# Convolution and whitening on one core: the DRAM scratch laid out by unit, the output stored as whole tiles

## The chip, the cores and the metric

The kernel runs on one core of a Trainium2 chip. The metric is device time in microseconds, from the start of the program to its end.

## The reference, cut to what matters

The input `x` is float32 of shape (4, 64, 256, 256): four images of 64 channels. Layer 0 is a long convolution: for each channel, a separable filter `hx * hy` (made by a small network of sines) is convolved with the 256 x 256 image by FFT with zero padding, and `x * bias` is added. Layer 1 whitens the 64 channels against each other:

```python
x1 = jnp.transpose(x, (1, 0, 2, 3)).reshape(64, -1)
x1_s = x1[:, ::9]                      # every ninth pixel
mean1 = jnp.mean(x1_s, axis=-1, keepdims=True)
cov = x1_s @ x1_s.T / x1_s.shape[1] + 0.01 * eye
deconv = isqrt_newton_schulz(cov, 5)
out = deconv @ (x1 - mean1)            # back to (4, 64, 256, 256)
```

Whitening needs the covariance of the whole result of layer 0 before its first output can be made, and that result (67 MB) doesn't fit on the core. So it goes to DRAM and comes back.

## The kernel before, in words

**Units.** The convolution is done in 128 units (`UNITS`), one for a channel `c` of one sweep; a sweep is two of the four images. A unit's input is a tile of 128 partitions x 1024 floats: partition `p` holds row `p` and row `128 + p` of both images (two images x two halves x 256 columns), which the host has put together, so `x[q]` is one contiguous 512 KB. On the partitions, the Toeplitz matrices of the filters are made from a Hankel load of 256 KB (L206 to L214). TensorE multiplies by the row filter (`make_v`) and then by the column filter (`make_y`), eight groups of matmuls for a unit in all (L593 to L603). VectorE adds `x * bias` and writes `y_sb[q % 2]`, one of only two buffers (L477, `finish_y`). From there, GpSimd masks every ninth pixel (L337), VectorE sums the groups (L485), and SyncE stores the tile to the scratch `convolved` (`y_dram`, L216 to L223).

**The waits on `y_sb`.** `finish_y(q)` waits until the store of unit `q - 2` has landed (`y_stored[k]`). SyncE's `load_x(q + 4)` waits until unit `q - 1` is done (L203); behind it on the same queue stand `store_y(q - 1)`, `load_hankel(q + 5)` and, from unit 68 on, `load_kept(q)`. All DMAs are issued by SyncE, so all stand in one hardware queue.

**Between.** After the last unit come the second half of the covariance on TensorE (L630), five Newton-Schulz steps (L552 to L671) and the whitening matrix `dmat`. DVE's last unit (L508 to L521) waits for the store of unit 125 (L516) and then works in two halves.

**Tiles.** The whitening runs over 64 tiles of 128 partitions x 2048 floats (1 MB). A partition is one channel of one half of an image, so `dmat` is block-diagonal with `deconv` twice. A tile is multiplied by `dmat` (L687), ScalarE and VectorE add the mean term from PSUM (L409, L578), and SyncE stores it. Fourteen tiles (`KEPT`) are loaded in the second sweep in four pieces each (L230 to L239), six more just after the last unit (L268 to L279), and the other 44 one by one as a slot comes free (L281 to L284). There are four output buffers.

**The scratch before.** `y_dram` has a row for each (image, half, channel), 128 x 256 floats, the rows of that half in order. A unit's store takes, from each partition, four runs of 1 KB (one for each image and half), and a tile's load takes 8 KB from each row. A tile's output is stored by two DMAs of 64 partitions (one for each half, L260 to L265), each partition to its place in the final array, 8 KB at a time.

The lines that the prediction's steps touch: L204 (x load), L214 (Hankel load), L223 (store of a unit), L239 (kept pieces), L258 (tile loads), L265 (output stores), L477 and L509 (VectorE's result of a unit), L516 (the wait for the store of unit 125), L598 to L601 (a group of matmuls), L630 (covariance), L687 (matmuls of a tile).

Of the kernel before, what the change touches and what calls it, by code (L numbers as in the profile page):

```python
# [6 lines left out]
F32 = mybir.dt.float32  # L7
# [36 lines left out]
ZW = 2 * C + 1  # L44
X_SLOTS, T_SLOTS, H_SLOTS = 5, 3, 3

TROWS = 8
TW = TROWS * S
TILES = B * (P // TROWS)
KEPT = 14  # L50
PIECES = 4
O_SLOTS = 4
MASK_COLS = 288


def conv_whiten(nc, x, first, hidden, columns, bias, out):
    g_dram = nc.dram_tensor("filters", [2 * C, GLEN], F32, kind="Internal").ap()
    y_dram = nc.dram_tensor("convolved", [B * HB * C, P * S], F32, kind="Internal").ap()

    with ExitStack() as ctx:  # L60
        def sb(name, shape, dt=F32):
# [96 lines left out]
        def wait(eng, s, value):  # L158
            if value > 0:
                eng.wait_ge(s, value)  # L160
# [27 lines left out]
        @block.sync  # L188
        def _(sp):
            sp.dma_start(first_sb, first).then_inc(params_loaded, 16)  # L190
            sp.dma_start(col[:], columns).then_inc(params_loaded, 16)

            sp.wait_ge(w_zeroed, 1)
            for k in range(2):
                h = slice(k * ORDER, (k + 1) * ORDER)
                sp.dma_start(w_sb[h, :, h], hidden[h, :].rearrange("p (l n) -> p l n", l=3)
                             ).then_inc(params_loaded, 16)

            def load_x(q):
                if q >= UNITS:  # L200
                    return

                wait(sp, y_done, q - X_SLOTS + 1)  # L203
                sp.dma_start(x_sb[q % X_SLOTS], x[q]).then_inc(x_loaded[q % X_SLOTS], 16)  # L204

            def load_hankel(q):  # L206
                if q >= UNITS:
                    return
                k = q % H_SLOTS

                wait(sp, flipped, q - H_SLOTS + 1)
                wait(sp, t_lo_done, q - H_SLOTS + 1)
                src = bass.AP(tensor=g_dram.tensor, offset=(q % C) * GLEN, ap=[[1, P], [C * GLEN, 2], [1, S]])
                sp.dma_start(hankel[k], src).then_inc(hankel_loaded[k], 16)  # L214

            def store_y(q):  # L216
                if q < 0:
                    return
                k = q % 2
                wait(sp, y_done, q + 1)  # L220
                dst = bass.AP(tensor=y_dram.tensor, offset=(q // C) * BLOCKS * C * P * S + (q % C) * P * S,
                              ap=[[S, P], [C * P * S, BLOCKS], [1, S]])
                sp.dma_start(dst, y_sb[k].rearrange("p (i w) -> p i w", w=S)).then_inc(y_stored[k], 16)  # L223

            def tile_in(t, lo, hi):
                image, rows = t // (P // TROWS), t % (P // TROWS)
                return bass.AP(tensor=y_dram.tensor, offset=image * HB * C * P * S + rows * TW + lo,
                               ap=[[P * S, HB * C], [1, hi - lo]])

            def load_kept(q):  # L230
                n = q - (C + 4)
                if not 0 <= n < KEPT * PIECES:
                    return
                w = TW // PIECES
                lo = n % PIECES * w

                for k in range(2):
                    sp.wait_ge(y_stored[k], 16 * (C // 2))
                sp.dma_start(kept[:, n * w:(n + 1) * w], tile_in(n // PIECES, lo, lo + w)).then_inc(kept_loaded, 16)  # L239

            for q in range(4):
                load_x(q)
            sp.dma_start(bias_sb[:], bias.to_broadcast([P, C])).then_inc(bias_loaded, 16)

            sp.wait_ge(filt_ready, 1)
            sp.dma_start(g_dram, filt).then_inc(filt_stored, 16)
            sp.wait_ge(filt_stored, 16)
            for q in range(5):
                load_hankel(q)

            for q in range(UNITS):
                load_x(q + 4)
                store_y(q - 1)
                load_hankel(q + 5)
                load_kept(q)

            def load_tile(t):
                sp.dma_start(t_in[t % slots], tile_in(t, 0, TW)).then_inc(t_loaded[t % slots], 16)  # L258

            def store_tile(t):  # L260
                image, rows, k = t // (P // TROWS), t % (P // TROWS), t % O_SLOTS
                for h in range(HB):
                    dst = bass.AP(tensor=out.tensor, offset=image * C * S * S + h * P * S + rows * TW,
                                  ap=[[S * S, C], [1, TW]])
                    sp.dma_start(dst, t_out[k][h * C:(h + 1) * C, :]).then_inc(t_stored[k], 16)  # L265


            sp.wait_ge(y_mm, UNITS)  # L268
            for t in range(KEPT, after_v):
                load_tile(t)  # L270
            store_y(LAST)
            for t in range(after_v, after_y):
                load_tile(t)
            for k in range(2):
                sp.wait_ge(y_stored[k], 16 * (UNITS // 2))
            sp.wait_ge(masked_done, LAST)
            sp.wait_ge(z_last_done, PER)
            for t in range(after_y, slots):
                load_tile(t)  # L279

            for t in range(TILES):  # L281
                if t + slots < TILES:
                    sp.wait_ge(t_mm[1], t + 1)
                    load_tile(t + slots)  # L284

                sp.wait_ge(t_act, t + 1)
                sp.wait_ge(t_dve, t + 1)
                store_tile(t)
            for k in range(O_SLOTS):
                sp.wait_ge(t_stored[k], 16 * HB * (TILES // O_SLOTS))  # L290

        @block.gpsimd
        def _(pool):
# [57 lines left out]
        @block.scalar  # L351
        def _(act):
            def flip(q):
                if q >= UNITS:
                    return
                k, h = q % T_SLOTS, q % H_SLOTS
                act.wait_ge(hankel_loaded[h], 16 * (q // H_SLOTS + 1))

                wait(act, y_mm, q - T_SLOTS + 1)
                nc.scalar.copy(t_f32[k], hankel[h][:, :, :P - 1:-1])  # L360
                nc.scalar.copy(t_hi[k], hankel[h][:, :, ::-1]).then_inc(flipped, 1)  # L361

            def round_x(q):
                if q >= UNITS:
                    return
                k = q % X_SLOTS
                act.wait_ge(x_loaded[k], 16 * (q // X_SLOTS + 1))

                wait(act, v_mm, q - 1)
                nc.scalar.copy(x_hi[q % 2], row_block(k, 0)).then_inc(x_hi_done, 1)  # L370

            def round_v(q):
                k = q % 2
                wait(act, v_mm, q + 1)

                wait(act, y_mm, q - 1)
                nc.scalar.copy(v_f32[k], ps_v[k][:, :, S:2 * S])  # L377

                nc.scalar.copy(v_hi[k], ps_v[k][:, :, 0:S]).then_inc(v_hi_done, 1)  # L379

            act.wait_ge(rate_ready, 1)
            nc.scalar.activation(decay, pos, ACT.Exp, scale=rate[:]).then_inc(decay_ready, 1)
            round_x(0)
            for layer in range(3):
                act.wait_ge(f_dve, layer + 1)
                nc.scalar.activation(hid, arg, ACT.Sin).then_inc(f_sin, 1)
            round_x(1)
            flip(0)
            flip(1)

            for q in range(UNITS):
                round_v(q)
                round_x(q + 2)
                flip(q + 2)

            act.wait_ge(filt_zeroed, 2)
            nc.scalar.activation(small[:, 7:8], small[:, 7:8], ACT.Sqrt)
            act.wait_ge(n_mm, 1)
            nc.scalar.activation(small[:, 1:2], ps[:, 0, 0:1], ACT.Sqrt).then_inc(n_act, 1)
            act.wait_ge(n_act, 1)  # L400
            nc.scalar.activation(small[:, 3:4], small[:, 1:2], ACT.Sqrt).then_inc(n_act, 1)
            act.wait_ge(d_ready, 1)

            for t in range(TILES):
                act.wait_ge(t_mm[0], t + 1)

                wait(act, t_stored[t % O_SLOTS], 16 * HB * (t // O_SLOTS))
                src = ps[:, bank(t, 0):bank(t, 0) + 2, :].rearrange("p r n -> p (r n)")
                nc.scalar.activation(t_out[t % O_SLOTS][:, 0:TW // 2], src, ACT.Identity,  # L409
                                     bias=small[:, 6:7]).then_inc(t_act, 1)  # L410

        @block.vector
        def _(dve):
# [159 lines left out]
            for t in range(TILES):  # L573
                dve.wait_ge(t_mm[1], t + 1)

                wait(dve, t_stored[t % O_SLOTS], 16 * HB * (t // O_SLOTS))
                src = ps[:, bank(t, 1):bank(t, 1) + 2, :].rearrange("p r n -> p (r n)")
                nc.vector.tensor_scalar(t_out[t % O_SLOTS][:, TW // 2:TW], src, small[:, 6:7], None, ALU.add  # L578
                                        ).then_inc(t_dve, 1)
# [139 lines left out]
```

## Time and profile before

| | us |
|---|---|
| median of 3 runs | 998.5 |
| lowest and highest | 994.86 and 1002.09 |
| the profiled execution | 994.94 |
| its span, first to last instruction | 993.1 |
| mean granted TensorE clock in it | 0.981 |

The rows below are in us of one profiled execution, counted from its first instruction. The span holds three stages: filters and ramp (0 to 41), the units (41 to 662), and from the last unit to the end (662 to 993). Of these the last holds the covariance and Newton-Schulz steps up to about 702, then the tiles. The chain of waits is one path only: what ended last, followed back.

### The profile page before, as it was taken

Reading aid. Unit: us, or ns where it says so; the run is one execution under the profiler, and the core shown is the slowest. Engines: PE = TensorE matmul, PEld = TensorE weight load, DVE = VectorE, ACT = ScalarE, POOL = GpSimd, SP = SyncE. Lnnn points to the kernel's source line nnn. Section 1 sums busy time; section 2 is a strip of 40 time slices with the busy share of each in tenths; the row PEclk is TensorE's granted clock in tenths of the full one; section 3 lists DMA queues with packets and bytes.
Section 4 is the critical chain, followed back from the end, with each engine's and each line's share of the span. In section 5 each row is a group of like instructions: output and inputs, shape, how many; then the busy total and the mean of one; then the engine's idle time right before and its main releaser. Section 6 shows DMA issues by size and latency. Waiting matters only on the chain.

```text
span 993.1 us, 15420 instructions
## 1 busy us (share of the span) xinstructions
PE 881.0 (89%) x5904; PEld 731.0 (74%) x5904; DVE 574.7 (58%) x642; ACT 397.8 (40%) x714; POOL 496.4 (50%) x277
## 2 busy tenths in 40 slices
PE   1799999999999999999999999977997777777896
PEld 0799999999999999999989899976432222222342
DVE  4487788778787657677767676771222222222332
ACT  2455555555555435454444444420121222222332
POOL 2488888889898747777767677760000000000000
PEclk9999999999999999999999999997799999999999
DMA  3799999999999959999999999975499999999999
GB/s 100 161 286 272 275 309 270 268 296 287 282 292 272 298 154 312 320 304 315 309 312 300 296 298 317 312 264 214 142 425 425 427 426 425 426 427 426 362 326 287
DMA packets 147301, 303.39 MB, mean 306 GB/s; under 512 B 10619, under 2 KB 109084, under 8 KB 132636
## 3 DMA queue, kind: packets, MB, share of 16 engines
q1 hardware_dynamic: 147228, 302.41, 92.1%
q8 instruction: 47, 0.77, 0.3%
q14 instruction: 26, 0.21, 0.1%
HBM read 167.96 MB, written 134.41 MB: 304 GB/s over the span
## 4 chain that ended last, share of the span: by engine, by line
PE 47%; DMA 41%; DVE 8%; SPq 2%; issue 1%; ACT 1%; POOL 0%; DVEq 0%; ACTq 0%
DMA convolved<-y_all 24%; DMA out<-z_all 14%; PE ps L601 12%; PE ps L687 10%; PE ps L598 7%; PE ps L599 7%; PE ps L600 7%; DVE y_all L477 4%; PE ps L630 3%; DMA out<-masked_all 2%; DVE z_all L578 1%; SPq L204 1%; ACT z_all L409 1%; DMA plain<-filters 0%; SPq L265 0%
## 5 line engine op out<-in xcount | busy, mean ns | idle before, releaser
L598 PE MATMUL ps<-rounded 128*128 128x256 f32 x1024 | 373.9, 365 | 24.6 <-issue 15.3
L337 POOL TENSOR_TENSOR masked_all<-y_all,mask 128x1024 f32<-128x1024 f32 x127 | 328.8, 2589 | 80.0 <-DVE y_all L477 79.7
L599 PE MATMUL ps<-rounded 128*128 128x256 f32 x1024 | 288.3, 282 | 0.0
L600 PE MATMUL ps<-rounded 128*128 128x256 f32 x1024 | 288.3, 282 | 0.0
L477 DVE SCALAR_TENSOR_TENSOR y_all<-x_all,bias_sb,ps 128x1024 f32<-128x1024 f32 x127 | 162.5, 1280 | 139.9 <-DMA convolved<-y_all 131.7
L598 PEld LDWEIGHTS ps<-rounded 128*128 128x128 f32 x1024 | 197.3, 193 | 30.7 <-issue 30.1
L308 POOL TENSOR_TENSOR rounded<-x_all,rounded 128x512 fp32r<-128x512 f32 x128 | 165.2, 1290 | 88.6 <-ACT rounded L370 87.4
L601 PE MATMUL ps<-plain,x_all 128*128 128x128 f32 x1024 | 197.9, 275 | 0.0
L599 PEld LDWEIGHTS ps<-rounded 128*128 128x128 f32 x1024 | 197.5, 193 | 0.0
L601 PE MATMUL ps<-plain 128*128 128x128 f32 x1024 | 196.7, 274 | 0.0
L600 PEld LDWEIGHTS ps<-rounded 128*128 128x128 f32 x1024 | 193.3, 189 | 0.0
L687 PE MATMUL ps<-kept,z_all 128*128 128x512 f32 x344 | 158.6, 612 | 33.3 <-ACT z_all L409 23.8
L601 PEld LDWEIGHTS ps<-plain,x_all 128*128 128x128 f32 x1024 | 158.2, 191 | 0.0
L687 PEld LDWEIGHTS ps<-kept,z_all 128*128 128x128 f32 x344 | 64.7, 194 | 126.3 <-issue 126.0
L601 PEld LDWEIGHTS ps<-plain 128*128 128x128 f32 x1024 | 157.3, 190 | 0.0
L370 ACT CAST rounded<-x_all 128x512 fp32r<-128x512 f32 x128 | 79.7, 622 | 193.0 <-DMA x_all<-x 193.0
L485 DVE TENSOR_REDUCE z_all<-masked_all 128x116 f32<-128x1044 f32 x127 | 156.7, 1234 | 0.0
L578 DVE TENSOR_SCALAR z_all<-ps,small 128x1024 f32<-128x1024 f32 x48 | 61.6, 1284 | 152.4 <-PE ps L687 94.5
L409 ACT ACTIVATE z_all<-ps,small 128x1024 f32<-128x1024 f32 x48 | 53.5, 1115 | 173.6 <-DMA out<-z_all 124.8
L377 ACT COPY plain<-ps 128x512 f32<-128x512 f32 x128 | 74.8, 584 | 105.5 <-PE ps L601 105.1
L466 DVE TENSOR_TENSOR rounded<-plain,rounded 128x512 fp32r<-128x512 f32 x128 | 93.2, 728 | 8.1 <-ACT rounded L361 8.1
L457 DVE TENSOR_TENSOR rounded<-ps,rounded 128x512 fp32r<-128x512 f32 x128 | 87.2, 681 | 14.0 <-ACT rounded L379 13.9
(98 smaller groups left out, 471.4 us busy)
## 6 DMA issues: line engine op xcount, KB each, us to landing
x_all<-x SPq DMA_DIRECT2D x128, 512.0 KB, 6.9
convolved<-y_all SPq DMA_DIRECT2D x128, 512.0 KB, 8.0
out<-z_all SPq DMA_DIRECT2D x96, 512.0 KB, 12.7
plain<-filters SPq DMA_DIRECT2D x128, 256.0 KB, 9.1
kept<-convolved SPq DMA_DIRECT2D x29, 1024.0 KB, 18.9
out<-masked_all SPq DMA_DIRECT2D x32, 512.0 KB, 12.8
kept<-convolved SPq DMA_DIRECT2D x56, 256.0 KB, 9.5
rounded<-convolved SPq DMA_DIRECT2D x9, 1024.0 KB, 18.8
```

The lines of the kernel that those rows point to most:

```text
L308: nc.gpsimd.tensor_tensor(x_lo[k], row_block(q % X_SLOTS, 0), x_hi[k].bitcast(F32), ALU.subtract).then_inc(x_lo_done, 1)
L337: nc.gpsimd.tensor_tensor(masked_of(k, 0, PER), by_image(y_sb[k]), mask_of(q // C, 0, PER), ALU.mult).then_inc(masked_done, 1)
L370: nc.scalar.copy(x_hi[q % 2], row_block(k, 0)).then_inc(x_hi_done, 1)
L457: nc.vector.tensor_tensor(v_lo[k], ps_v[k][:, :, 0:S], v_hi[k].bitcast(F32), ALU.subtract).then_inc(v_lo_done, 1)
L466: nc.vector.tensor_tensor(t_lo[k], hankel[h][:, :, ::-1], t_hi[k].bitcast(F32), ALU.subtract).then_inc(t_lo_done, 1)
L477: nc.vector.scalar_tensor_tensor(y_sb[k], x_sb[q % X_SLOTS], bias_sb[:, q % C:q % C + 1], ps_y[k].rearrange("p a n -> p (a n)"), ALU.mult, ...
L485: nc.vector.tensor_reduce(z_of(q % C), grouped(q % 2, 0, BLOCKS), AX_X, ALU.add).then_inc(z_done, 1)
L598: mm(wide, hi[:, b, cols], t_hi[k][:, f, :], start=True, stop=False)
L599: mm(wide, hi[:, b, cols], t_lo[k][:, f, :], start=False, stop=False)
L600: mm(wide, lo[:, b, cols], t_hi[k][:, f, :], start=False, stop=False)
L601: last = mm(o[:, b, m * S + P:(m + 1) * S], block1[:, b, cols], t_f32[k][:, f, :], start=False, stop=True)
L687: last = mm(ps[:, bank(t, u) + r, :], dmat, t_in[k][:, w:w + IMG], start=True, stop=True)
```

## The change

Three things change, all of them layouts in DRAM. The scratch now has 256 rows of 64 x 1024 floats (256 KB): a row stands for 64 consecutive partitions of one unit, and within it each partition's 1024 floats stand together. A unit's store is one DMA, whose DRAM side has the pattern of counts 2, 64, 1024 in place of 128, 4, 256. A tile is now two partitions' share of all units of a sweep: partition `(h, c)` of the tile holds channel `c` and two neighbouring rows of the partition half `h`. It is loaded from 128 rows at 8 KB each, as before in size. The output array of the kernel is `[64, 128, 2048]`, each tile stored by one DMA as one contiguous megabyte, and the host puts it in order at the end. The kept tiles come in 28 pieces of 512 KB (4 KB for a partition) in every second unit, in place of 56 pieces of 256 KB in every unit. The number of tiles, their size and all arithmetic are the same; the sum over channels still runs over the partitions of a half.

```diff
-TROWS = 8
-TW = TROWS * S
-TILES = B * (P // TROWS)
+ROWS = P // 2
+TROWS = 2
+TW = TROWS * XW
+SWEEP_TILES = ROWS // TROWS
+TILES = SWEEPS * SWEEP_TILES
 KEPT = 14
-PIECES = 4
+PIECES = 2
...
-    y_dram = nc.dram_tensor("convolved", [B * HB * C, P * S], F32, kind="Internal").ap()
+    y_dram = nc.dram_tensor("convolved", [SWEEPS * P, ROWS * XW], F32, kind="Internal").ap()
...
-                dst = bass.AP(tensor=y_dram.tensor, offset=(q // C) * BLOCKS * C * P * S + (q % C) * P * S,
-                              ap=[[S, P], [C * P * S, BLOCKS], [1, S]])
-                sp.dma_start(dst, y_sb[k].rearrange("p (i w) -> p i w", w=S)).then_inc(y_stored[k], 16)
+                dst = bass.AP(tensor=y_dram.tensor, offset=((q // C) * P + q % C) * ROWS * XW,
+                              ap=[[C * ROWS * XW, 2], [XW, ROWS], [1, XW]])
+                sp.dma_start(dst, y_sb[k]).then_inc(y_stored[k], 16)
 
             def tile_in(t, lo, hi):
-                image, rows = t // (P // TROWS), t % (P // TROWS)
-                return bass.AP(tensor=y_dram.tensor, offset=image * HB * C * P * S + rows * TW + lo,
-                               ap=[[P * S, HB * C], [1, hi - lo]])
+                sweep, rows = t // SWEEP_TILES, t % SWEEP_TILES
+                return bass.AP(tensor=y_dram.tensor, offset=sweep * P * ROWS * XW + rows * TW + lo,
+                               ap=[[ROWS * XW, P], [1, hi - lo]])
 
             def load_kept(q):
-                n = q - (C + 4)
-                if not 0 <= n < KEPT * PIECES:
+                n = (q - (C + 4)) // 2
+                if q % 2 or not 0 <= n < KEPT * PIECES:
                     return
...
             def store_tile(t):
-                image, rows, k = t // (P // TROWS), t % (P // TROWS), t % O_SLOTS
-                for h in range(HB):
-                    dst = bass.AP(tensor=out.tensor, offset=image * C * S * S + h * P * S + rows * TW,
-                                  ap=[[S * S, C], [1, TW]])
-                    sp.dma_start(dst, t_out[k][h * C:(h + 1) * C, :]).then_inc(t_stored[k], 16)
+                sp.dma_start(out[t], t_out[t % O_SLOTS]).then_inc(t_stored[t % O_SLOTS], 16)
...
-    out = nc.dram_tensor("out", [B, C, S, S], F32, kind="ExternalOutput").ap()
+    out = nc.dram_tensor("out", [TILES, P, TW], F32, kind="ExternalOutput").ap()
...
-    return r.results[0]["out"]
+    tiles = r.results[0]["out"].reshape(SWEEPS, SWEEP_TILES, 2, C, TROWS, PER, HB, S)
+
+    return np.ascontiguousarray(tiles.transpose(0, 5, 3, 6, 2, 1, 4, 7)).reshape(B, C, S, S)
```

The waits on `t_stored` (L290, L407, L576) count one store for each tile in place of two.

## Rows read from the trace of the kernel before

**Rows 1.** Windows: us, busy time and count of each engine, granted clock, DMA share, GB/s

```profile
41.00:341.00 300.00, 300.00 (x2601) 299.91 (x2600) 239.26 (x259) 165.33 (x325) 261.98 (x130) 1.00 0.98 282
365.00:645.00 280.00, 264.36 (x2212) 259.29 (x2210) 199.26 (x221) 135.41 (x276) 201.36 (x111) 0.99 1.00 309
684.00:702.00 18.00, 10.61 (x33) 7.68 (x34) 5.79 (x25) 0.37 (x2) 0.00 (x0) 0.57 0.01 2
730.00:920.00 190.00, 142.95 (x309) 55.87 (x307) 49.39 (x39) 42.88 (x39) 0.00 (x0) 0.99 1.01 426
930.00:985.00 55.00, 55.00 (x128) 24.09 (x128) 20.52 (x16) 18.95 (x17) 0.00 (x0) 1.00 0.98 320
```

**Rows 2.** Windows of line L477 alone: us, DVE busy (count), clock, DMA share, GB/s

```profile
41.00:141.00 100.00, 26.99 (x22) 1.00 0.99 280
...
365.00:465.00 100.00, 25.62 (x20) 1.00 1.01 314
465.00:565.00 100.00, 24.33 (x19) 0.98 1.00 303
565.00:645.00 80.00, 20.49 (x16) 1.00 0.99 309
```

**Rows 3.** The chain of waits, 592 to 668 us: start, length, what

```profile
594.03 8.76 DMA convolved<-y_all
602.80 0.02 issue
602.82 1.29 DVE y_all L477
604.13 0.35 SPq L204
604.48 0.05 issue
604.53 8.62 DMA convolved<-y_all
...
662.35 0.66 DVE y_all L509
...
667.23 15.88 PE ps L630 x116
```

**Rows 4.** The page's DMA queue: packets, MB, share of 16 engines

```profile
q1 hardware_dynamic: 147228, 302.41, 92.1%
```

**Rows 5.** The page's DMA issues: count, KB each, median us to landing

```profile
x_all<-x SPq DMA_DIRECT2D x128, 512.0 KB, 6.9
convolved<-y_all SPq DMA_DIRECT2D x128, 512.0 KB, 8.0
plain<-filters SPq DMA_DIRECT2D x128, 256.0 KB, 9.1
```

**Rows 6.** DMA in the window 5 to 12 us, in 40 slices (x loads, 4 KB runs)

```profile
GB/s 47 187 281 374 281 328 351 304 304 374 421 421 445 421 468 398 398 398 421 374 468 421 468 398 398 421 421 374 343 170 143 94 117 117 117 94 45 37 12 0
```

**Rows 7.** The store of a unit: issues and time to landing

```profile
L223 SPq DMA_DIRECT2D convolved<-y_all x128: 360/434/1462, 41.0 to 665.4; - x128
DMA to landing us min/median/max: 2.9/8.0/12.1
```

**Rows 8.** The chain of waits at the ramp, 30 to 60 us: two groups of matmuls apart, early and late

```profile
31.05 0.43 PE ps L601 x2
32.11 0.43 PE ps L601 x2
...
45.40 0.22 PE ps L601 x2
45.98 0.22 PE ps L601 x2
```

More of the change, by code:

```diff
@@ L289, in _ @@
             for k in range(O_SLOTS):
-                sp.wait_ge(t_stored[k], 16 * HB * (TILES // O_SLOTS))
+                sp.wait_ge(t_stored[k], 16 * (TILES // O_SLOTS))
         @block.gpsimd
@@ L405, in _ @@
                 act.wait_ge(t_mm[0], t + 1)
-                wait(act, t_stored[t % O_SLOTS], 16 * HB * (t // O_SLOTS))
+                wait(act, t_stored[t % O_SLOTS], 16 * (t // O_SLOTS))
                 src = ps[:, bank(t, 0):bank(t, 0) + 2, :].rearrange("p r n -> p (r n)")
@@ L574, in _ @@
                 dve.wait_ge(t_mm[1], t + 1)
-                wait(dve, t_stored[t % O_SLOTS], 16 * HB * (t // O_SLOTS))
+                wait(dve, t_stored[t % O_SLOTS], 16 * (t // O_SLOTS))
                 src = ps[:, bank(t, 1):bank(t, 1) + 2, :].rearrange("p r n -> p (r n)")
```

## The prediction

> **What bounds the kernel now.** I read the windows by stage first, then the counts of L477 (one for each unit) in the same stages, then the chain of waits, and last the DMA page.
>
> In the first sweep TensorE never stops: 300.00 us busy of 300, and the DMA share is 0.98 at 282 GB/s [rows 1]. A unit takes 4.6 us: a group of matmuls starts every 0.58 us, eight times over is 4.6 [rows 8], and 22 units in 100 us agree [rows 2]. In the second sweep the kept tiles are loaded beside the units, and TensorE is busy 264.36 of 280 us [rows 1]. Between 365 and 645 us there are 20 + 19 + 16 = 55 units, 5.09 us each [rows 2]. The chain says what holds them: the landing of a store, VectorE's 1.29 us that waited for its buffer, SyncE's 0.35 us, and again a store of 8.6 to 8.8 us [rows 3]. Two such buffers alternate, so a unit costs half of that ring. The engines of the DMA are full (share 1.00 at 309 GB/s [rows 1]), where 426 GB/s went through with 8 KB runs [rows 1]: 1 KB runs are the reason.
>
> From the last unit's first half (662.35) to the end is 331 us [rows 3]. Of these the tiles take nearly 290: DMA-bound at 426 GB/s until near 930, then TensorE-bound, 16 tiles of eight matmuls in 55 us [rows 1].
>
> **The change part by part.**
>
> *Runs of the unit's store, 1 KB to 4 KB.* By bytes alone this frees the DMA. 128 descriptors replace 512. A unit moves 1.31 MB (512 + 512 + 256 KB [rows 5]), at 282 GB/s 4.65 us; if the two big transfers went at the 421 GB/s of the x loads [rows 6] and only the 256 KB at 282, it would be 2.49 + 0.93 = 3.4 us, under TensorE's 4.6. That is the gain the edit offers if all else is equal, and it could be had only in the second sweep: 55 x (5.09 - 4.61) = 26 us.
>
> *The shape of the store.* All else isn't equal. The DRAM side's outermost count goes from 128 to 2, while the SBUF side stays 128 partitions. The question is over how many of the 16 DMA engines such a transfer is spread. The trace has no store like it, but it has one count that shows that the number can be below 16. Queue 1 moved 147228 packets [rows 4]. Data packets, one for each contiguous run, are 16384 (x) + 65536 (unit stores) + 32768 (Hankel) + 7168 (kept pieces) + 6400 (50 tiles) + 8192 (outputs) + 128 (filters out) + 33 (network input, 33 rows) + 128 + 384 + 128 (columns, hidden weights, bias) = 137249. That leaves 9979 for completions. The 624 DMAs at 16 each would make 9984. Five are missing, which is what the one DMA with 33 rows would leave if it ran on 11 engines, the largest divisor of 33 up to 16. So I read: the engines take equal shares of the outermost count, and a count that 16 doesn't divide gets fewer of them. Each side must be cut so, and 2 can be cut in two only. The two shares are 64 partitions each, 256 KB.
>
> The Trainium skill says this outright (DMA: Bandwidth & Descriptors, "Why a DMA increments its semaphore by 16 and not by 1"): the number of engines is the largest one up to 16 that divides the slowest non-1 count of both patterns. By that rule the store runs on 2; by the rule of thumb that long runs are better it would be a gain. The completion count agrees with the former for the 33 rows, but no run here yet shows it for two sides with different outer counts.
>
> *Cost on two engines.* The 16 engines pass 426 GB/s with 8 KB runs [rows 1], 26.6 each; in the window of 4 KB loads the full slices are near 421 [rows 6], 26.3 each. So the store of a unit takes 262144 B / 26.3 GB/s = 10.0 us on each of its two. The same two also carry their sixteenth of everything else: x 32768 B, 1.25 us; Hankel 16384 B in 1 KB runs, at something between 17.6 (282/16) and 26.3 GB/s, I take 22, 0.75 us. Sum 12.0 us for a unit against 4.6. The other fourteen engines are idle most of this time. Kept pieces add 32768 B, 1.25 us, 28 times: 35 us (the 56 smaller pieces before were the same bytes).
>
> Does anything hide it? TensorE's 4.6 us (8.5 at the ramp's slow pitch, 8 x 1.06 [rows 8]) and VectorE, ScalarE and GpSimd fit in 12. Nothing but the two buffers stands between the store and the chain: `finish_y(q)` waits for store q - 2, while store q - 1 is in the queue, so the two engines never run dry (the answer to a landing, 1.29 + 0.35 us plus the issue, is far shorter than a store). The new bound is those engines' throughput, not a latency. x and Hankel loads stand in the same queue behind the store and come late too, but five x slots and three Hankel slots cover one store.
>
> *Sum.* The first store is issued at 41.0 [rows 7]. The last wait on a store in this stage is L516, for the store of unit 125, the 126th. Up to its landing: 126 x 10.0 = 1260, 124 x loads x 1.25 = 155, 123 Hankel loads x 0.75 = 92, kept 35. 41 + 1542 = 1583. Then the rest as before, 331: 1914 (the 2 stores still in the queue then, 20 us on two engines, delay tiles 14 to 20, for which nobody asks before 14 kept tiles are used up). TensorE is busy a third of the time now, and its clock may stand lower: in the 18 us of small steps at 684 us it was 0.57 [rows 1]. The covariance of 15.88 us [rows 3] may take up to twice that; I take half of it, 8. With 1.9 us outside the span, and a few us for the two engines' gaps, 1930. The bounds: 26.6 GB/s for everything gives 11.7 us for a unit, about 1890, and engines somewhat quicker when fourteen are idle are not excluded; the 17.6 GB/s of the mixed first sweep for all bytes would give 17.5 us a unit (the last rival), but there most runs were 1 KB, so I go a third of the way, to 2150. 994.94 was 3.6 under the median; that is nothing here.
>
> *Kept pieces* every second unit, 4 KB runs in place of 2 KB: same bytes, half the issues, 0 to -5 us under the old bound, nothing under the new one.
>
> *Tile loads*: 8 KB runs as before, 256 KB apart in place of 128. The output stores before had just that pitch and ran within the 426 GB/s mix [rows 1]. Zero; at worst, the 44 loads' 46 MB at the second sweep's 309 GB/s in place of 426, 149 - 108 = 41 us. I take the end to which the row of the pitch belongs, 0.
>
> *Output stores*: one DMA for a tile in place of two, contiguous, 128 partitions outermost on both sides, so all 16 engines. SyncE issues 64 fewer. The stage is bound by bytes at 426 and then by TensorE, so 0; the store that ends the kernel is 1 MB either way. -2 to +2.
>
> **The rivals.**
>
> *Fast: the store is spread over 16 engines all the same* (patterns split again before they reach the chip, or the cut taken from the SBUF side alone). For it: the pattern says the same thing to a program that would split 64 again. Against it: the missing five completions. Then DMA demand is 3.4 us a unit plus 0.6 for kept pieces, TensorE sets the pace in both sweeps, and the time is 995 - 26 = 969, perhaps 973 with landing waits left over. It decides as soon as the busiest engine needs less than TensorE's 4.6 us for a unit; on four engines that would still be 5.0 + 2.0. 13%.
>
> *No change: 16 engines, but the rate of the units is set by reading and writing DRAM at once*, not by the runs. For it: the share is full at 309 GB/s beside TensorE, VectorE and all [rows 1]. Against it: loads and stores in the tile stage mix too, and pass 426 [rows 1]. The ring of two buffers then keeps its 8.6 to 8.8 us [rows 3], the unit its 5.09, and the time is 995. 6%, half of it a gain of some us over 1%.
>
> *Slower still*: two engines, and each passes only the 17.6 GB/s of the mixed first sweep. 17.5 us for a unit, 126 x 5.5 = 690 more, 2620. It is the far end of the forecast's own case, with little weight since its runs are long.
>
> **How the numbers follow.** Slow case 81%, fast 13%, little change 6%. The predicted time is 1930, and 1800 to 2150 takes in the bounds of the engines' rate and the clock; the 19% of the other cases are left out. This kernel's measurement tells about 1% from no change. Faster by over 1%: 0.15; within 1%: 0.04; slower: 0.81.
>
> **What would show it.** The median of `convolved<-y_all` to landing goes from 8.0 to over 20 us (two stores in the queue). L477 starts every 12 us, its idle time released by that DMA on nearly all of 127. The DMA share in the unit stages falls to about (2 x 12 + 14 x 2) / (16 x 12) = 0.27, GB/s to 110; queue 1's completions fall by 128 x 14 = 1792 packets, and by 1024 more for the 64 output DMAs and 448 for the 28 kept ones that go. The tiles still run at 426. The chain is nearly all `DMA convolved<-y_all` up to 1580. I'm wrong if the share in the units stays near 0.8 with landings under 8 us.

## The result, and the profile after

The changed kernel takes 1897.66 us (median of 4 runs, 1896.63 to 1898.15) against 997.81: ratio 1.901, 95% interval 1.894 to 1.908. Predicted were 1930, and 1800 to 2150.

The windows of the kernel after, with the columns of [rows 1]; the first three are of the units, then the small steps before the tiles, then the tiles:

```profile
41.00:341.00 300.00, 177.95 (x1065) 173.88 (x1063) 92.39 (x103) 66.62 (x132) 103.56 (x52) 0.80 0.41 112
365.00:645.00 280.00, 163.08 (x946) 159.39 (x946) 86.10 (x96) 60.27 (x120) 95.91 (x48) 0.78 0.37 111
700.00:1500.00 800.00, 450.24 (x2707) 440.19 (x2706) 233.91 (x261) 162.90 (x324) 238.33 (x130) 0.78 0.43 124
...
1592.00:1610.00 18.00, 10.26 (x32) 7.41 (x32) 6.18 (x26) 0.37 (x2) 0.00 (x0) 0.57 0.40 147
1640.00:1840.00 200.00, 151.86 (x335) 60.04 (x334) 53.94 (x42) 46.71 (x42) 0.00 (x0) 1.00 1.01 427
```

The DMA passes 112 GB/s where it passed 282, and TensorE's clock stands near 0.8. The tiles run at 427 GB/s as before. The whole loss is in the units. How often VectorE finishes one, in the window 60 to 335 us, and what it waited for over the whole run (us of idle time, number of times):

```profile
L476 DVE SCALAR_TENSOR_TENSOR y_all<-x_all,bias_sb,ps x23: 1279/1281/1283, 66.3 to 328.4; 128x1024 f32<-128x1024 f32 x23
```

```profile
  DMA convolved<-y_all: 1055.0, 124
```

22 intervals in 262.1 us: 11.91 us a unit, where the kernel before had 4.64 in the same window. The chain of waits, which answers to [rows 3]:

```profile
520.49 22.02 DMA convolved<-y_all
542.51 0.03 issue
542.54 1.29 DVE y_all L476
543.83 0.02 issue
543.85 0.34 SPq L207
544.19 0.04 issue
544.24 22.04 DMA convolved<-y_all
...
1571.41 0.76 DVE y_all L508
...
1576.29 15.42 PE ps L629 x116
```

A store takes 22 us to land and not 8.6, and two buffers share it: (22.02 + 1.29 + 0.34 + 0.09) / 2 = 11.9. From the last unit's first half (1571.41) to the end of the span (1895.6) it is 324 us, 7 fewer than before. The page's queue, which answers to [rows 4], and its issues:

```profile
q1 hardware_dynamic: 91228, 302.40, 48.7%
...
convolved<-y_all SPq DMA_DIRECT2D x128, 512.0 KB
...
plain<-filters SPq DMA_DIRECT2D x128, 256.0 KB, 21.9
```

The same bytes in 56000 fewer packets. Data packets are now 137249 - 49152 (unit stores) - 3584 (kept pieces) = 84513, so 6715 are completions, as the prediction calls the packets that carry no data. 532 DMAs at 16 would make 8512; the 33-row load leaves out its 5 again, and 1792 more are missing: exactly 14 for each of the 128 stores.

### The profile page after: what moved, and what is told of

Read it like the earlier page. It is cut to its first block, busy times and chain, and to the rows that moved or that the text cites. A ratio compares the mean times of both kernels' runs of the same rounds, so it can differ in the third digit from the quotient of the medians.

```text
span 1895.6 us, 15300 instructions
## 1 busy us (share of the span) xinstructions
PE 1141.6 (60%) x5904; PEld 979.2 (52%) x5904; DVE 568.6 (30%) x642; ACT 399.9 (21%) x714; POOL 491.0 (26%) x277
## 3 DMA queue, kind: packets, MB, share of 16 engines
q1 hardware_dynamic: 91228, 302.40, 48.7%
## 4 chain that ended last, share of the span: by engine, by line
DMA 84%; PE 7%; DVE 6%; SPq 2%; issue 1%; ACT 0%; DVEq 0%; ACTq 0%
DMA convolved<-y_all 74%; DMA out<-z_all 9%; PE ps L686 4%; DVE y_all L476 4%; SPq L207 2%; PE ps L629 1%; DVE z_all L577 1%; PE ps L600 0%; DVE kept L436 0%; DMA plain<-filters 0%; ACT z_all L408 0%; PE ps L665 0%; PE ps L597 0%; PE ps L669 0%; PE ps L598 0%
## 5 line engine op out<-in xcount | busy, mean ns | idle before, releaser
L597 PE MATMUL ps<-rounded 128*128 128x256 f32 x1024 | 475.1, 464 | 652.0 <-issue 638.6
L597 PEld LDWEIGHTS ps<-rounded 128*128 128x128 f32 x1024 | 267.7, 261 | 672.3 <-issue 667.4
L476 DVE SCALAR_TENSOR_TENSOR y_all<-x_all,bias_sb,ps 128x1024 f32<-128x1024 f32 x127 | 162.6, 1280 | 1056.1 <-DMA convolved<-y_all 1055.0
L598 PE MATMUL ps<-rounded 128*128 128x256 f32 x1024 | 355.1, 347 | 0.0
L599 PE MATMUL ps<-rounded 128*128 128x256 f32 x1024 | 353.1, 345 | 0.0
L600 PE MATMUL ps<-plain,x_all 128*128 128x128 f32 x1024 | 297.4, 390 | 0.0
L598 PEld LDWEIGHTS ps<-rounded 128*128 128x128 f32 x1024 | 269.9, 264 | 0.0
L599 PEld LDWEIGHTS ps<-rounded 128*128 128x128 f32 x1024 | 263.8, 258 | 0.0
L600 PEld LDWEIGHTS ps<-plain,x_all 128*128 128x128 f32 x1024 | 256.0, 305 | 0.0
L600 PE MATMUL ps<-plain 128*128 128x128 f32 x1024 | 207.1, 285 | 0.0
L600 PEld LDWEIGHTS ps<-plain 128*128 128x128 f32 x1024 | 171.2, 205 | 0.0
L465 DVE TENSOR_TENSOR rounded<-plain,rounded 128x512 fp32r<-128x512 f32 x128 | 87.9, 687 | 8.1 <-ACT rounded L360 8.1
```

The lines of the kernel that those rows point to most:

```text
L465: nc.vector.tensor_tensor(t_lo[k], hankel[h][:, :, ::-1], t_hi[k].bitcast(F32), ALU.subtract).then_inc(t_lo_done, 1)
L476: nc.vector.scalar_tensor_tensor(y_sb[k], x_sb[q % X_SLOTS], bias_sb[:, q % C:q % C + 1], ps_y[k].rearrange("p a n -> p (a n)"), ALU.mult, ...
L597: mm(wide, hi[:, b, cols], t_hi[k][:, f, :], start=True, stop=False)
L598: mm(wide, hi[:, b, cols], t_lo[k][:, f, :], start=False, stop=False)
L599: mm(wide, lo[:, b, cols], t_hi[k][:, f, :], start=False, stop=False)
L600: last = mm(o[:, b, m * S + P:(m + 1) * S], block1[:, b, cols], t_f32[k][:, f, :], start=False, stop=True)
```

## The experiments

The kernel before ran beside each group; its median was 991.45, 995.24 and 992.96 us in the three. Ratios are against it, with a 95% interval. Times of a unit are worked out as above, from the first and last start of VectorE's result of a unit (L477, or L476 to L479 by the kernel) in the windows 60 to 335 us (first sweep) and 370 to 640 us (second). With 2 and 4 parts the second sweep starts later than that, so only the first window is given for them. The code cuts leave out the waits, whose counts follow the number of stores and buffers. Where one time is given alone, the kernel ran once.

**Two DMAs of 64 partitions.** The changed kernel, scratch and runs as they are.

```diff
-                dst = bass.AP(tensor=y_dram.tensor, offset=((q // C) * P + q % C) * ROWS * XW,
-                              ap=[[C * ROWS * XW, 2], [XW, ROWS], [1, XW]])
-                sp.dma_start(dst, y_sb[k]).then_inc(y_stored[k], 16)
+                for h in range(2):
+                    dst = bass.AP(tensor=y_dram.tensor, offset=((q // C) * P + h * C + q % C) * ROWS * XW,
+                                  ap=[[XW, ROWS], [1, XW]])
+                    sp.dma_start(dst, y_sb[k][h * ROWS:(h + 1) * ROWS, :]).then_inc(y_stored[k], 16)
...
```

> The changed kernel with one edit: a unit's store is two DMAs, one for each half of 64 partitions, so that the outermost count is 64 on both sides. Scratch layout, run length (4 KB), bytes and tiles are the same. Theory A (the time is lost to the number of engines that the outermost count allows): all 16 engines take part, TensorE sets the pace of the units, L477's counterpart starts every 4.6 to 4.7 us, and the time is 960 to 980 us. Theory B (the new scratch layout is slow to write, a 256 KB stretch for each half in one place): the time stays within 5% of 1898 us, landings near 20 us.

991.61 us, ratio 0.9999 (0.9973 to 1.0025). The loss is gone with this one edit, so neither the layout nor the run length was to blame. Queue 1's 95068 packets hold 10555 completions, all that 660 DMAs make but the 5 of the 33-row load: all 16 engines took part in each half. But the gain that I expected (960 to 980) isn't there: 4.76 us a unit in the first sweep and 5.08 in the second.

**The scratch in 4, 8 and 16 parts.** The store is one DMA again; only the outermost count of its DRAM side differs (its offset, the tile loads and the host's order follow).

```diff
-ROWS = P // 2
+PARTS = 4
+ROWS = P // PARTS
...
-                              ap=[[C * ROWS * XW, 2], [XW, ROWS], [1, XW]])
+                              ap=[[C * ROWS * XW, PARTS], [XW, ROWS], [1, XW]])
...
```

> The changed kernel with the scratch cut into 4 parts of 32 partitions in place of 2 of 64: the store is still one DMA of 4 KB runs, its DRAM pattern has the counts 4, 32, 1024. Theory A: four engines carry 128 KB each, 5.0 us for the store by the 12.08 - 2.0 us that two engines took for twice as much, 7.0 us a unit with their share of the x and Hankel loads (7.3 with kept pieces), so 41 + 127 x 7.1 + 331 = 1270 to 1300 us. 12 completion packets are missing for each store, 1536 in all. Theory B (layout, or something that goes by the run length or the number of descriptors): within 5% of 1898. A third, that any outermost count under 128 is handled by 2 engines: 1898.

> The changed kernel with 8 parts of 16 partitions, pattern 8, 16, 1024: eight engines carry 64 KB each. Theory A (busiest engine's throughput): 4.83 us was the difference between 2 and 4 engines, 128 KB a unit; so 64 KB fewer gives 6.94 - 2.4 = 4.5 us in the first sweep, where TensorE's 4.61 takes over, and 7.57 - 2.4 = 5.2 in the second. Total 995 to 1015 us, with 8 completions missing for each store. Rival (the landing latency of a store on two buffers is what binds, and it doesn't fall with bytes): over 1100.

> The changed kernel with the scratch in 16 parts of 8 partitions: one DMA, counts 16, 8, 1024. Theory A: 16 engines, no completions missing, DMA demand 3.3 to 3.9 us for a unit, TensorE-bound at 4.6: 960 to 980 us, the same as with two DMAs of 64 within 3 us. Theory B: near 1898, or if the stretch of 256 KB mattered, something between.

| outermost count | total, us | a unit, first sweep | queue 1's packets | completions missing for a store |
|---|---|---|---|---|
| 2 (the change) | 1897.66 | 11.91 | 91228 | 14 |
| 4 | 1283.17 | 6.92 | 91484 | 12 |
| 8 | 1040.09 | 5.09 | 91996 | 8 |
| 16 | 976.35 | 4.62 | 93020 | 0 |

16 parts: ratio 0.9852 (0.9811 to 0.9893). The row of L477 with 4 parts, and with 16:

```profile
L477 DVE SCALAR_TENSOR_TENSOR y_all<-x_all,bias_sb,ps x39: 1279/1280/1282, 66.1 to 329.1; 128x1024 f32<-128x1024 f32 x39
```

```profile
L477 DVE SCALAR_TENSOR_TENSOR y_all<-x_all,bias_sb,ps x60: 1269/1281/1283, 62.4 to 334.8; 128x1024 f32<-128x1024 f32 x60
```

For 2, 4, 8 and 16 the number of engines is the outermost count, and the missing completions count the idle ones; the pace of the units follows it. The times with 4 and with 8 parts are of one run each. Four parts came out as expected. Eight did not: 1040 where I had 995 to 1015, 5.09 us where the busiest engine's sum gave 4.5. Its chain in the first sweep:

```profile
203.49 8.51 DMA convolved<-y_all
212.03 1.29 DVE y_all L477
213.72 8.16 DMA convolved<-y_all
```

(8.51 + 1.29 + 0.4) / 2 = 5.1: the chain goes around the ring of two buffers, and its landings of 8.2 to 8.5 us are longer than the near 7.3 (2 x 4.5 less 1.7) that the busiest engine's sum would make them. The last experiment comes back to that.

**The output alone.** The kernel before with the tiles stored whole.

```diff
...
-                for h in range(HB):
-                    dst = bass.AP(tensor=out.tensor, offset=image * C * S * S + h * P * S + rows * TW,
-                                  ap=[[S * S, C], [1, TW]])
-                    sp.dma_start(dst, t_out[k][h * C:(h + 1) * C, :]).then_inc(t_stored[k], 16)
+                sp.dma_start(out[t], t_out[t % O_SLOTS]).then_inc(t_stored[t % O_SLOTS], 16)
...
```

> The kernel before with one part of the change alone: the output goes out as whole tiles of 1 MB by one DMA, ordered by the host; scratch and unit stores as before. My theory: nothing, 0 to -3 us against before, as the tiles are bound by bytes at 426 GB/s and then by TensorE. The rival: contiguous megabytes and half the DMAs raise the rate or shorten the end, over 10 us faster.

988.07 us, ratio 0.996 (0.9938 to 0.9981): 4 us gained (2 to 6), a little more than I had. SyncE's issues at the end show a part of it, the kernel before first and then this one:

```profile
986.45 1.80 SPq L265 DMA_DIRECT2D out<-masked_all x2
```

```profile
981.04 0.33 SPq L261 DMA_DIRECT2D out<-masked_all x1
```

The last store is out after 0.33 us and not after 1.80, and the span ends 4.0 us behind this issue's end where it was 4.8. Whether one DMA or the contiguous megabyte does it wasn't tried apart.

**The kept pieces alone**, in the kernel before:

```diff
-PIECES = 4
+PIECES = 2
...
-                n = q - (C + 4)
-                if not 0 <= n < KEPT * PIECES:
+                n = (q - (C + 4)) // 2
+                if q % 2 or not 0 <= n < KEPT * PIECES:
```

> The kernel before with the kept pieces alone changed: 28 of 512 KB in every second unit in place of 56 of 256 KB. I expect 0 to -5 us: the bytes are the same, the runs 4 KB in place of 2 KB save 56 x 16 KB x (1/24.4 - 1/25.8) / engine, some 2 us, and SyncE issues less. A rival: the burst of 512 KB delays the unit stores behind it, +5 us or more.

993.67 us, ratio 0.9971 (0.9945 to 0.9996). As expected, next to nothing; the 24.4 and 25.8 GB/s from which the 2 us were reckoned stand in no run of this case.

**What two DMAs cost.** First the kernel before with each store in two halves of the partitions:

```diff
...
+                for h in range(2):
+                    at = (q // C) * BLOCKS * C * P * S + (q % C) * P * S + h * 64 * S
+                    dst = bass.AP(tensor=y_dram.tensor, offset=at, ap=[[S, 64], [C * P * S, BLOCKS], [1, S]])
+                    src = y_sb[k][h * 64:(h + 1) * 64, :].rearrange("p (i w) -> p i w", w=S)
+                    sp.dma_start(dst, src).then_inc(y_stored[k], 16)
...
```

> The kernel before with a unit's store as two DMAs of 64 partitions each, 1 KB runs and scratch as before. It asks why two DMAs of 64 gained nothing in the changed kernel where one of 128 gained 15 us. Theory H (a transfer from one half of the partitions uses a part of the ways out of SBUF, so the sixteen engines wait for each other): slower than before by 10 to 20 us, first sweep at 4.75 us a unit. Theory N (it was the number of DMAs and SyncE's issue time, 0.45 us each): slower by less than 5 us here, since the queue is full anyway; and the next run is slower than one DMA by 10 us or more.

1031.02 us, ratio 1.0344 (1.029 to 1.0397): 4.93 and 5.38 us a unit, where the kernel before has 4.64 and 5.14. The loss is larger than either theory had. Then the 16 parts with each store in two halves of the columns:

```diff
...
-                sp.dma_start(dst, y_sb[k]).then_inc(y_stored[k], 16)
+                for h in range(2):
+                    at = ((q // C) * PARTS * C + q % C) * ROWS * XW + h * (XW // 2)
+                    dst = bass.AP(tensor=y_dram.tensor, offset=at,
+                                  ap=[[C * ROWS * XW, PARTS], [XW, ROWS], [1, XW // 2]])
+                    sp.dma_start(dst, y_sb[k][:, h * (XW // 2):(h + 1) * (XW // 2)]).then_inc(y_stored[k], 16)
...
```

> The version with 16 parts, with a unit's store as two DMAs, each of all 128 partitions and half the columns (2 KB runs). Theory H (halves of the partitions): within 5 us of the one-DMA version's 976, since both DMAs use all partitions; 2 KB runs cost a little. Theory N (number of DMAs): 990, as with two DMAs of 64 partitions.

996.84 us, ratio 1.0017 (0.9983 to 1.0052): 4.77 and 5.07 us a unit, the same as with two halves of the partitions. So a second DMA costs the gain, whichever way the tile is cut, and theory H isn't needed. (The halves of the columns also have runs of 2 KB, which no run tried with one DMA.) Its chain:

```profile
408.97 0.70 SPq L229
...
409.70 7.19 DMA convolved<-y_all
...
416.92 1.29 DVE y_all L479
...
418.23 0.33 SPq L208
...
418.61 0.52 SPq L229
```

SyncE's first issue (0.52 to 0.70 us) now stands in the ring ahead of the second store, near 0.6 us for two units. That is enough for the 0.15 and 0.22 us by which units are slower than with one DMA (4.62 and 4.85), but it was argued from the chain and not tried alone. Why the old layout loses 34 us by the same cut stays open.

**Three buffers.** What is left of a store's landing is told from the engines' throughput by a third buffer for a unit's result. It takes 4 KB of each partition, so 13 tiles are kept and not 14; a control has that alone.

```diff
-KEPT = 14
+KEPT = 13
...
+Y_SLOTS = 3
...
-                wait(dve, y_stored[k], 16 * (q // 2))
+                wait(dve, y_stored[q % Y_SLOTS], 16 * (q // Y_SLOTS))
...
```

> The version with 16 parts, with three buffers for a unit's result in place of two, and 13 kept tiles in place of 14 to make room. Theory L (with 16 engines a store is a latency: landing 7 to 8 us plus 1.7 us of VectorE and SyncE, spread over two buffers, is what holds the second sweep at 4.82 us a unit): with three buffers TensorE alone sets the pace, 4.61 to 4.65, 54 x 0.2 = 10 us fewer there; the tile that is no longer kept adds 2.5 us of loading. 966 to 972 where the two-buffer version has 976. Theory T (the engines are full, share 0.98): 4.8 as before and 977 to 980.

> The control for it: 16 parts, two buffers, 13 kept tiles. One tile more to load in the bytes-bound stage, 1 MB at 426 GB/s, 2.5 us; a little less in the second sweep. 976 to 980 us.

> 8 parts with three buffers and 13 kept tiles. It asks why 8 engines took 5.09 us for a unit in the first sweep where the sum of the busiest engine is 4.5. Theory L (the ring of two buffers: the landing has a part that doesn't shrink with the bytes): 4.6 to 4.7 us in the first sweep, 5.1 in the second, about 1000 us. Theory T (the busiest engine passes less than I reckon beside other traffic): 5.0 to 5.1 as before, 1035 to 1045.

> The changed kernel itself (2 parts, two engines) with three buffers and 13 kept tiles. My prediction said that the bound is the two engines' throughput and not a latency: then a third store in the queue changes nothing, 11.9 us for a unit in the first sweep and 1890 to 1905 us. The rival, that it is the landing of a store over two buffers: a third fewer, 8 us for a unit, near 1450.

| parts | buffers | total, us | ratio | a unit, first sweep |
|---|---|---|---|---|
| 16 | 2, 13 kept | 980.72 | 0.9868 (0.9829 to 0.9908) | 4.64 |
| 16 | 3 | 970.51 | 0.9774 (0.9753 to 0.9795) | 4.64 |
| 8 | 3 | 993.35 | one run | 4.64 |
| 2 | 3 | 1886.86 | one run | 11.91 |

What VectorE waited for with 16 parts and 13 kept tiles, two buffers first, then three:

```profile
  DMA convolved<-y_all: 84.1, 58
  PE ps L601: 31.3, 51
```

```profile
  PE ps L602: 49.4, 82
```

And the row with 2 parts and three buffers, which is that of the changed kernel again:

```profile
L477 DVE SCALAR_TENSOR_TENSOR y_all<-x_all,bias_sb,ps x23: 1279/1280/1283, 65.8 to 327.9; 128x1024 f32<-128x1024 f32 x23
```

With two engines a third buffer changes nothing in the pace: it is throughput. The 11 us that this run is shorter (3 below what I expected) lie at the end of the stage: with three buffers the last unit waits for store 124 and not 125, and starts at 1560.0 us and not at 1571.4. With eight and with sixteen engines the third buffer takes the store out of VectorE's waits, and the first sweep runs at 4.64 us: there the landing over two buffers was what held eight.

The control with 13 kept tiles came 0.7 us above the range that I had for it.

In the second sweep eight engines go from 5.51 to 5.16 us a unit and no further. VectorE waits for no store there; the longest waits from 470 to 640 us are ScalarE's for the x load:

```profile
ACT rounded L371 <- DMA x_all<-x: 92.0, 33, 3.9
```

The busiest of eight needs 4.5 us and 0.6 for its share of a kept piece, 5.1 in all. So here it is most likely throughput again, though no run told it apart. With 16 parts the second sweep goes from 4.88 (the control with 13 kept tiles; 4.85 with 14) to 4.70 us a unit, and the version beats both kernels, the kernel before by 2.3% and the changed one by half.

## Why the prediction was right, point by point

- *The shape of the store.* Right. Two engines, shown by the 14 missing completions, by 4, 8 and 16 parts, and by two DMAs of 64. The rule of the Trainium skill (DMA: Bandwidth & Descriptors, "Why a DMA increments its semaphore by 16 and not by 1") holds here for two sides with different counts (2 and 128), which no row of before could show.
- *Cost on two engines.* Right in kind and size: 12.0 us was forecast for a unit without kept pieces, 11.91 measured, the same with three buffers. The sum up to store 125 was 1583, measured 1571. With kept pieces a unit took 12.43 us, 0.5 more, where the 35 us over 64 units had made it 0.55.
- *The engines' rate.* Going from 2 to 4 engines takes 128 KB off the busiest, and 11.91 - 6.92 = 4.99 us: 131072 B / 4.99 us = 26.3 GB/s, the rate that was taken from the full slices of [rows 6].
- *Sum.* 1930 was 32 us too long. 12 of it are the stage of the units, 7 the tail (324 and not 331), 8 the covariance, for which I had added half its length: it took 15.42 us, not more than before, though the clock was lower in the units. The rest is the few us for gaps that weren't there. All four lay on the same side, so nothing cancelled. One reading in the sum was wrong and cost nothing: TensorE wasn't busy a third of the time but 59% (177.95 of 300 us), as its matmuls were longer at the lower clock (L597 464 ns each, L598 before 365). That still fits in 11.91 us.
- *Output stores.* -2 to +2 was a little too narrow: -4 (-6 to -2). From the last unit to the end it is 325.5 us with this part alone and 324.2 in the changed kernel, where it was 330.8, so by these profiles most of the 7 us are this part's.
- *Kept pieces and tile loads.* Right: -3 us (-5 to 0), and 427 GB/s with rows 256 KB apart.
- *1 KB runs as the reason for 282 and 309 GB/s.* The runs don't bear this out. With 16 parts the stores have runs of 4 KB, and the same windows show nearly the same share at nearly the same rate:

```profile
41.00:341.00 300.00, 300.00 (x2604) 300.00 (x2603) 240.23 (x260) 166.29 (x325) 261.67 (x131) 1.00 0.96 283
365.00:645.00 280.00, 272.50 (x2319) 269.33 (x2317) 210.38 (x232) 142.44 (x287) 211.36 (x116) 1.00 0.98 320
```

By the 3.4 us of DMA demand in 4.6 the first share would have been near 0.74. So a share near 1 in the units didn't say that the engines could pass no more; why it is so high isn't shown. It cost the forecast nothing, since two engines set the pace.
- *The fast rival* was priced at 969 if all 16 engines took part. That case, made by 16 parts, has 976: the units gain 13 us where I had 26. The step of this rival that failed is "TensorE sets the pace in both sweeps": in the second, 13 us of waits on landings stayed, where I had left 4, and three buffers take most of that away (4.88 to 4.70 us a unit).
- *What would show it.* The 0.27 for the DMA share was wrong: 0.37 to 0.41 at the 110 GB/s that I had. With the two engines full, 0.37 to 0.41 leaves the other fourteen busy for 3.3 to 3.9 us of a unit, not the 2 that their bytes make at the rate of [rows 6]. The share couldn't be worked out from the bytes; what lengthens the packets isn't shown. The landings, 124 waits of 127 and the number of packets came as written. The median landing of these stores isn't on the page; the chain has it.

## What to carry to other kernels

Before lengthening runs, look at the outermost count on both sides of the DMA: here it, and not the 128 partitions on the other side, decided how many engines carried the store. If a layout wants a short outermost count, cut the scratch so that it becomes 16; one DMA of count 16 was better here than two of count 64 (976 against 992 us). And the completions in a queue's packet count (packets less data packets, against 16 for each DMA) tell without any other view whether a transfer ran on all engines.

## What the runs showed that I had not expected

A DMA's issue can hold its engine long. SyncE's timeline in the changed kernel, where the Hankel load took 0.46 us to issue before (the median; 2.11 at most):

```profile
508.22 0.35 SPq L207 DMA_DIRECT2D x_all<-x  x1
508.61 0.52 SPq L226 DMA_DIRECT2D convolved<-y_all  x1
509.24 7.64 SPq L217 DMA_DIRECT2D plain<-filters  x1
```

7.64 us for an issue behind two queued stores on two engines, which is also the median of all 128. It costs nothing here: the issue ends at 516.88 us, and the next x load waits for VectorE until 520.1 anyway. With three buffers it comes into the chain, 6.58 us of the Hankel load's issue at 509.83 us, and the pace is still 11.91. That a queue full on two engines holds the issue for all sixteen is my reading; no run tried it alone.
